# Reordering the opening of a fused attention and mixture-of-experts kernel: block-diagonal keys by one product, six staging rooms for the shared weights

## The reference, cut to what matters

```python
x = x + tanh(g_xattn[0]) * xattn(layernorm(x), ctx, ctx, W_q, b_q, W_k, b_k, W_v, b_v, W_o, b_o)
x = x + tanh(g_ffn[0]) * ffn(layernorm(x), ln_g, ln_b, Wr, W1, W3, W2, W1s, W3s, W2s)

# xattn
scores = einsum('bhsd,bhtd->bhst', qh, kh) / sqrt(16)
attn = einsum('bhst,bhtd->bhsd', softmax(scores), vh)      # then W_o and b_o
# ffn
h = layernorm(x, ln_g, ln_b)
gates, idx = top 2 of softmax(h @ Wr)                       # routed part, capacity 732 slots per expert
shared = silu(h @ W1s) * (h @ W3s) @ W2s
out = routed + shared
```

## Time and profile before

| | |
|---|---|
| time, median of 3 runs | 896.01 us (895.62 to 900.38) |
| profiled execution, its own time | 895.07 us |
| its span from first to last instruction | 893.3 us |
| PE busy | 832.9 us, 93% |
| DVE busy | 587.8 us, 66% |
| ACT busy | 387.7 us, 43% |
| POOL busy | 329.8 us, 37% |
| mean granted TensorE clock | 0.982 of full |

### The profile page before, as it was taken

How to read it: one execution, slowest core, us unless ns; L and a number is a source line. 1 busy time by engine, 2 the same in 40 slices (tenths; PEclk the granted TensorE clock), 3 DMA queues, 4 the chain that set the end, 5 groups by cost and what they waited for, 6 DMA issues and landing times.

```text
span 893.3 us, 14663 instructions
## 1 busy us (share of the span) xinstructions
PE 832.9 (93%) x5262; PEld 725.7 (81%) x5262; DVE 587.8 (66%) x1284; ACT 387.7 (43%) x717; POOL 329.8 (37%) x251
## 2 busy tenths in 40 slices
PE   8788999999989999999998999999999999999990
PEld 7464876858857778588587899999999999999990
DVE  4576769777588686795777577565666757565340
ACT  4336345363353442633525245453544445353330
POOL 4841203232032230230225812818466481814333
PEclk9899999999999999999899999999999999999995
DMA  6641310422204114131032422434444333431111
GB/s 222 163 111 34 94 37 25 119 48 62 71 25 117 18 37 112 36 78 31 24 118 72 139 83 62 94 106 88 83 111 91 99 61 87 100 65 20 18 19 19
DMA packets 93985, 66.94 MB, mean 75 GB/s; under 512 B 55110, under 2 KB 80892, under 8 KB 93928
## 3 DMA queue, kind: packets, MB, share of 16 engines
q1 hardware_dynamic: 40312, 55.40, 21.9%
q0 software_dynamic: 53088, 10.30, 8.4%
q10 hardware_dynamic: 528, 0.52, 0.2%
HBM read 37.38 MB, written 14.27 MB: 58 GB/s over the span
## 4 chain that ended last, share of the span: by engine, by line
PE 70%; DVE 12%; issue 6%; ACT 3%; POOL 2%; DVEq 0%; POOLq 0%; ACTq 0%
PE bank L1574 19%; PE bank L1575 18%; PE bank L1576 18%; PE bank L1802 2%; DVE row_max L1260 2%; PE bank L1803 2%; PE bank L1804 2%; PE bank L1664 2%; PE bank L1692 2%; DVE hidden L1343 1%; ACT float_data L1080 1%; DVE hidden L1278 1%; PE bank L1698 1%; PE bank L1844 1%; PE bank L1767 1%
## 5 line engine op out<-in xcount | busy, mean ns | idle before, releaser
L1574 PE MATMUL bank<-split_operands 128*128 128x366 f32 (+4 forms) x1148 | 382.0, 333 | 9.3 <-DVE float_data L1296 4.4
L1575 PE MATMUL bank<-split_operands 128*128 128x366 f32 (+4 forms) x1148 | 376.3, 328 | 0.0
L1576 PE MATMUL bank<-split_operands 128*128 128x366 f32 (+4 forms) x1148 | 376.1, 328 | 0.0
L1574 PEld LDWEIGHTS bank<-split_operands 128*128 128x128 f32 (+1 forms) x1148 | 214.5, 187 | 29.4 <-issue 8.2
L1576 PEld LDWEIGHTS bank<-split_operands 128*128 128x128 f32 (+1 forms) x1148 | 214.1, 186 | 12.1
L1575 PEld LDWEIGHTS bank<-split_operands 128*128 128x128 f32 (+1 forms) x1148 | 214.5, 187 | 9.5
L998 POOL DMA_INDIRECT out<-float_data,scatter_now x42 | 125.4, 2987 | 179.6 <-DVE float_data L1537 97.6
L1557 DVE TENSOR_TENSOR hidden<-bank,float_data 128x366 f32<-128x366 f32 x112 | 60.5, 540 | 114.1 <-PE bank L1576 114.1
L1179 ACT ACTIVATE float_data<-bank 128x366 f32<-128x366 f32 x112 | 53.5, 478 | 113.7 <-PE bank L1576 113.7
L1176 ACT CAST split_operands<-hidden 128x366 fp32r<-128x366 f32 x112 | 55.7, 497 | 68.3 <-DVE hidden L1557 68.3
L973 POOL DMA_INDIRECT float_data<-z_scratch,gather_now x42 | 72.2, 1720 | 14.8 <-issue 14.2
(11 more groups left out here) (157 smaller groups left out, 1066.8 us busy)
## 6 DMA issues: line engine op xcount, KB each, us to landing
float_data<-in_L_ffn_W SPq DMA_DIRECT2D x21, 1024.0 KB, 8.3
split_operands<-split_operands SPq DMA_DIRECT2D x96, 128.0 KB, 2.3
float_data<-in_x SPq DMA_DIRECT2D x8, 512.0 KB, 4.6
z_scratch<-float_data SPq DMA_DIRECT2D x8, 512.0 KB, 3.2
out<-float_data SPq DMA_DIRECT2D x7, 512.0 KB, 2.9
split_operands<-split_operands SPq DMA_DIRECT2D x8, 192.0 KB, 3.8
float_data<-in_L_ffn_W1s SPq DMA_DIRECT2D x2, 512.0 KB, 9.5
float_data<-in_L_ffn_W3s SPq DMA_DIRECT2D x2, 512.0 KB, 7.8
```

What stands on the lines that cost most here:

```text
L1574: pe.matmul(o, lhs[0], rhs[0], start=first, stop=False)
L1575: pe.matmul(o, lhs[0], rhs[1], start=False, stop=False)
L1576: return pe.matmul(o, lhs[1], rhs[0], start=False, stop=last)
```

## The change

In words, all in the opening:

- The eight DMAs of `first_keys` that fill `kbd`, and POOL's clearing of `kbd`, go. In their place POOL builds a 128 x 8 mask `own_head` with three small instructions (1 where the row belongs to the head), and DVE writes all of `kbd` by one product of the keys with the mask (`spread_keys`, 1232 columns), after `transpose_x` of block 0.
- Each of the six halves has a room of its own: `prob[2]`, `prob[3]`, `gf` and three in the float area. Halves 3 to 5 are issued without waits (`more_shared`), right behind the key stores and ahead of the `kst` reads.
- ACT rounds all twelve shared pieces in one run before the maxima are done. Two runs of pieces, of four and of two, leave their places between the exponentials and behind `attention_hi`. POOL takes the first six remainders ahead of `residual`, the other six behind the second block's statistics and values, and then `residual` of block 0. `residual` of block 1 and `route_const` move behind `attention_lo`.
- `stats_x` of block 1 comes ahead of `values_out`.
- `project_values` moves from between the maxima 2 and 3 to behind them. Maxima 0 waits for the hi part of the queries (`qh_ready`) and the product, no longer for the lo part; the banks of even and odd tiles are exchanged.
- New waits: the exponentials 2 and 3, the first DVE step of `scores` and `project_out` each wait for the POOL remainders that still read their room.

```diff
@@ def first_period(do, b):
     do("bias_keys")
+    do("more_shared")
     do("transpose_x", b)
+    do("spread_keys")
...
-    do("residual", b)
     do("stack", b)
-    do("shared_weights")
+    do("shared_hi", 0, 6)
+    do("shared_lo", 0, 6)
     for t in range(TT):
         do("maxima", b, t)
         if t == 1:
             do("keep_busy", 6, 4, "xl_ready", KD)
-        if t == 2:
-            do("project_values")
+    do("project_values")
...
-    do("more_shared")
+    do("stats_x", n)
     do("values_out")
-    norm(do, n)
+    do("shared_lo", 6, NPIECE)
+    do("scale_x", n)
+    do("residual", b)
     do("first_scores", b)
     do("transpose_x", n)
-    do("route_const")
     do("scores", b, 0)
-    do("shared_hi", 3, 5)
-    do("shared_lo", 6, 10)
...
     do("project", b)
-    do("shared_hi", 5, 6)
-    do("shared_lo", 10, NPIECE)
+    do("residual", n)
+    do("route_const")
     do("project_out", b)
@@ build
-    sh_stage = [af(kb, WCOLS // 2) for kb in (32, 40, 28, 32, 40, 44)]
+    sh_stage = [v.rearrange("p a n -> p (a n)") for v in (prob[2], prob[3], gf)] + \
+        [af(kb, WCOLS // 2) for kb in (32, 40, 28)]
+    own_head = sb("rows_of_head", [P, 8])
@@ sync, first_keys
-            sp.wait_ge(sig["zeros_ready"], 1)
-            sp.wait_ge(sig["k_hi"], KD)
-            for j in range(8):
-                sp.dma_start(kbd[16 * j:16 * j + 16, :, j, :].bitcast(F32), k_s[16 * j:16 * j + 16, 0, :, 0:SK].bitcast(F32))\
-                  .then_inc(sig["kbd_loaded"], 16)
             sp.wait_ge(sig["k_lo"], KD)
@@ vector
+        def spread_keys():
+
+            dve.wait_ge(sig["heads_ready"], 1)
+            dve.wait_ge(sig["k_hi"], KD)
+            dve.tensor_tensor(kbd, k_s[:, 0, :, 0:SK].bitcast(F32).unsqueeze(2).broadcast_to([P, KD, 8, SK]),
+                              own_head[:, :].unsqueeze(1).unsqueeze(3).broadcast_to([P, KD, 8, SK]), ALU.mult)\
+               .then_inc(sig["kbd_spread"], 1)
@@ tensor, maxima of block 0
-                    pe.wait_ge(sig["ql_ready"], KD)
-                    pe.wait_ge(sig["kbd_loaded"], 128)
+                    pe.wait_ge(sig["qh_ready"], KD)
+                    pe.wait_ge(sig["kbd_spread"], 1)
```

More of the change, by code:

```diff
@@ L464, in max_banks @@
     if b.at(0):
-        return (0, 1, 2) if t % 2 else (3, 4, 5)
+        return (3, 4, 5) if t % 2 else (0, 1, 2)
     if b.at(1):
@@ L651, in build @@
     stage_loaded = [sig["stage_loaded0"], sig["stage_loaded1"]]
-    shared_loaded = [sig[f"shared_loaded{j}"] for j in range(3)]
+    shared_loaded = [sig[f"shared_loaded{j}"] for j in range(6)]
     x_loaded = [sig["x_loaded0"], sig["x_loaded1"]]
@@ L704, in _, with load_shared @@
         sp.dma_start(xb[1], x_rows[1]).then_inc(x_loaded[1], 16)
-        def load_shared(h):
-            if h >= 3:
-                sp.wait_ge(sig["wsplit_lo"], NSTEP0 + 2 * (h - 2))
-            if h == 5:
-                sp.wait_ge(sig["xT_ready"], 2 * KD)
-            m, part = h // 2, h % 2
-            kk = wsv[m].shape[1] // 2
-            sp.dma_start(sh_stage[h].rearrange("p (k f) -> p k f", k=kk), wsv[m][:, part * kk:(part + 1) * kk])\
-              .then_inc(shared_loaded[h % 3], 16)
-        for h in range(3):
-            load_shared(h)
-        def first_keys():
-            sp.wait_ge(sig["zeros_ready"], 1)
-            sp.wait_ge(sig["k_hi"], KD)
-            for j in range(8):
-                sp.dma_start(kbd[16 * j:16 * j + 16, :, j, :].bitcast(F32), k_s[16 * j:16 * j + 16, 0, :, 0:SK].bitcast(F32))\
-                  .then_inc(sig["kbd_loaded"], 16)
+        def load_shared(first, last):
+            for h in range(first, last):
+                m, part = h // 2, h % 2
+                kk = wsv[m].shape[1] // 2
+                sp.dma_start(sh_stage[h].rearrange("p (k f) -> p k f", k=kk), wsv[m][:, part * kk:(part + 1) * kk])\
+                  .then_inc(shared_loaded[h], 16)
+        load_shared(0, 3)
+        def first_keys():
             sp.wait_ge(sig["k_lo"], KD)
@@ L731, in more_shared @@
         def more_shared():
-            for h in range(3, 6):
-                load_shared(h)
+            load_shared(3, 6)
         def load_keys(b):
@@ L744, in load_keys @@
                           .then_inc(sig["kbd_loaded"], 16)
+                if b.at(0):
+                    sp.wait_ge(sig["zeros_ready"], 1)
                 sp.wait_ge(sig["k_stored"], 32)
@@ L833, in _ @@
                            pattern=[[-1, P]], channel_multiplier=1).then_inc(sig["ident_ready"], 1)
-        do(pool.memset(kbd.bitcast(F32), 0.0))
+        do(pool.memset(own_head[:, :], 1.0))
+        do(pool.affine_select(out=own_head[:, :], in_=own_head[:, :], compare_op=ALU.is_ge, fill=0.0, base=0,
+                              pattern=[[-DH, 8]], channel_multiplier=1))
+        pool.affine_select(out=own_head[:, :], in_=own_head[:, :], compare_op=ALU.is_ge, fill=0.0, base=DH - 1,
+                           pattern=[[DH, 8]], channel_multiplier=-1).then_inc(sig["heads_ready"], 1)
         kneg = kst[96:112].rearrange("p a b t -> p (a b) t")
@@ L980, in first_gather @@
             gather(Turn(0, 1))
-        token_blocks(pool, {"stats_x": stats_x, "residual": residual, "weights": weights, "shared_weights": shared_weights,
+        token_blocks(pool, {"stats_x": stats_x, "residual": residual, "weights": weights,
                             "shared_lo": split_shared, "values_out": first_values, "scores": attention_lo, "stack": stationary_values, "norm2": norm2,
@@ L1037, in split_shared @@
         def split_shared(h):
-            act.wait_ge(shared_loaded[h % 3], 16 * (h // 3 + 1))
+            act.wait_ge(shared_loaded[h], 16)
             for j in range(2):
@@ L1043, in split_shared, with shared_hi @@
                    .then_inc(sig["wsplit_hi"], 1)
-        def shared_weights():
+        def shared_hi(first, last):
             act.activation(tgx[:, :], gx, ACT.Tanh).then_inc(sig["tanh_done"], 1)
             act.activation(tgf[:, :], gy, ACT.Tanh).then_inc(sig["tanh_done"], 1)
-            for h in range(3):
-                split_shared(h)
-        def shared_hi(first, last):
             for h in range(first, last):
@@ L1075, in exps @@
                 act.wait_ge(sig["wsplit_lo"], NSTEP0)
+            if b.at(0) and (p == 2 or p == 3):
+                act.wait_ge(sig["wsplit_lo"], NSTEP0 + 2 * (p - 1))
             act.wait_ge(sig["scores_ready"], b.n * NPAIR + p + 1)
@@ L1270, in scores @@
             dve.wait_ge(sig["z_stored"], b.n * 16)
+            if b.at(0):
+                dve.wait_ge(sig["wsplit_lo"], NSTEP0 + 6)
             if b.at(1):
@@ L1637, in maxima @@
                     pe.wait_ge(sig["k_lo"], KD)
+                    pe.wait_ge(sig["qh_ready"], KD)
+                    pe.wait_ge(sig["kbd_spread"], 1)
+                elif t == 1:
                     pe.wait_ge(sig["ql_ready"], KD)
-                    pe.wait_ge(sig["kbd_loaded"], 128)
-                elif t >= 2:
+                else:
                     pe.wait_ge(sig["m_done"], t - 1)
```

17 lines of the change are left out of this document (6 added, 11 removed).

## The result

| | before | after |
|---|---|---|
| median | 899.79 us (893.31 to 903.35, 22 runs) | 905.6 us (899.07 to 909.65, 22 runs) |
| ratio to before | | 1.0063, 95% interval 1.0039 to 1.0086 |
| profiled execution, its own time | 895.07 us, span 893.3 | 906.02 us, span 904.3 |
| mean granted clock in it | 0.982 | 0.970 |

The account below looks back on a forecast made before the run. The prediction took the opening's first scores on PE to be bound by SP's issue list, not by the maxima. It summed -2.4 us there and 0 for all else, from a median of 896.0 to 893.6 us, range 890.7 to 896.6.

Parts of the forecast that it names:

- T: Start of the first scores on PE, bound by SP's issue list: from 34.99 to 32.6 us, 2.4 earlier.
- Rival 2: New weight loads move in among the key stores, landing at 20.0 to 21.7: gain 0.9 to loss 0.8 us; chance 0.12.
- rival 1: Key stores land undisturbed at 17.1: gain 3.8 us, or 5.1 if the code load falls away too; chance 0.28.
- Rival 4: PE's slow clock lasts through the twelve query matmuls after the first scores: +2.9 us, 896.5; chance 0.03.
- cover: Rounded maxima ready at about 27.5, 1.5 us earlier and 2.7 before SP wants them: worth nothing.
- The product for `kbd`: On DVE after 14.6: 2.0 to 5.7 us, taken as 3, ending ahead of the hi queries; nothing reaches T.
- The casts: Four weight pieces, 2.18 us, leave ACT's place between the exponentials: worth 0.
- the step on POOL: Six remainders, block 1's normalisation at 30.4 instead of 35.4, six more until 36.8, residual until 39.6: slack, worth 0.
- + 0 (all else): Everything in the change besides the earlier first scores, summed as 0 us.
- My rival for the other side: The slower case: new loads delay the key stores, slower from a landing after 20.93, loss up to 0.8 us; chance 0.12.

Follow-up runs that it names:

- e4: Kernel before with only the block-diagonal keys changed (mask, one DVE product, eight copies gone), weight loads and pieces as before: 899.4 us, ratio to before 1.0028.
- e9: Kernel of e1 with only the first of six weight halves issued ahead of the key stores, the other five behind: 900.36 us, ratio to before 1.0000.
- e5: Kernel of e1 with 22 instead of 8 identity products on PE ahead of the first scores: 898.37 us, ratio to before 0.9992.
- e6: Kernel before with 27 instead of 8 identity products in PE's gap ahead of the first scores: 898.77 us, ratio to before 1.0019.
- e1: Changed kernel with POOL waiting for DVE's normalisation of block 1 before the second six weight remainders: 894.18 us, ratio to before 0.9975.
- e3: Changed kernel with POOL waiting for its own instruction behind each of the second six weight remainders: 899.56 us, ratio to before 1.0009.
- e8: Changed kernel with POOL's train cut after two of its ten instructions, waiting there for DVE's normalisation: 899.9 us in one run.
- e7: Changed kernel with PE's idle time ahead of the first scores and of block 1's transposes filled with identity products: 904.58 us, ratio to before 1.0058.
- e2: Changed kernel with block 1's normalisation as scalar_tensor_tensor with two tensor inputs, same order: 906.54 us, ratio to before 1.0074.
- e10: Kernel of e9 with 13 instead of 8 identity products ahead of the first scores: 898.37 us, ratio to before 0.9992.

## Why the prediction was wrong

**Right: what bounds T, and its size.** The reads were to start at 18.5 (17.8 to 19.5), it was 19.11; from there to T 14.06, it was 14.27, with one long issue in it as before (1.66 us at 21.39, again among the `kst` reads and not, as I had it, among the queries); T 32.6, it was 33.38. Rival 2 (new loads delay the stores) has e4 against it, rival 1 (undisturbed stores) e4 and e9. Rival 4 didn't come: the slow clock ended at about 43.6, and block 1's query products from 47.20 on ran at 1.00. The Trainium skill's rule on the order in which a DMA engine takes its descriptors ("DMA: Bandwidth & Descriptors", section "Queues, rings and completion order"), cited in the prediction, isn't contradicted: with loads issued behind them the stores took 5.8 to 6.8 us to the first read, without them 5.97.

**Right: cover and zeros.** The maxima were rounded at 28.07 (27.5), 2.9 us ahead of their copy. The product for `kbd` took 2.43 us (3, within 2.0 to 5.7) and held nobody. The casts are worth nothing (e5 against e6). And with POOL held back, in e1, the rest of the sum came out: first scores 2.1 us earlier than before, `project` 2.4, the time 0.25% less, 2.2 us against the 2.4 forecast, in an interval that just reaches no change.

**Wrong: the step on POOL.** It says that the statistics put first give "the normalised block at 30.4, not 35.4. Its transposes run behind the first scores, so this is slack too. Then six more until 36.8 and the residual". Start and end of POOL's train were right to about 0.5 us (29.93 to 37.31, then to 40.03); the start of the normalisation to 0.65 (29.65). What failed is its duration: I kept 1.38 us from a trace in which POOL was idle at that moment, and laid it beside ten POOL instructions. Two paragraphs above, for the `kbd` product, I had read from the earlier trace rows that a DVE instruction of 0.42 us takes 1.18 with POOL beside it. I used it there as a factor by columns, for the instruction that was new, and not for the instruction that was moved. The runs show it isn't a factor here: the normalisation, which works from SBUF to SBUF, waits for the end of what POOL runs, one instruction if POOL pauses behind it (e3), the whole train if it doesn't (e8, after). So this wait was 0 in the sum, part of its "+ 0 (all else)", and should have been: train end 40.03, less the 35.3 at which PE was free for the transposes, 4.7; measured 5.03.

The sum then: T 1.6 earlier; transposes 3.55 later than before, not 1.6 earlier, since they hang on POOL's train and no longer on T; `project` 4.1 later (58.30 against 54.22). The rest up to the measured 5.8 us I put down to the clock, which is argued and not shown: the fall in `project` costs 2.3 us where it comes, so 4.1 to 6.4 with it, but it comes with the old order too (e6), and how often in either kernel isn't known. The 10 us at 0.50 around the wait cost little (e7). In the two profiled executions the falls make the difference look like 11 us.

**The chances.** "Slower by more than 0.5%" had 0.02, and no rival of mine named a mechanism on POOL. My rival for the other side lay in the part that I had studied most. The order rows in front of the prediction show what it takes to see it: POOL's residual, which waited for the normalisation, had left its place between the statistics and the remainders, and with it went a wait that had kept the two engines apart by accident.

The Trainium skill states such a rule on the page "SBUF — State Buffer", section "SBUF: two separate sides": DVE and GpSimd share a pair of ports by an exclusive lock, which whichever starts first keeps for its whole instruction while the other stands still; DVE needs it in a two-port mode, and with two SBUF inputs when the GpSimd instruction reads SBUF. The trace agrees on who is held: L1236 and e2's form are, the reductions from PSUM are not. It doesn't give how long: with the pair kept for one instruction and then free, the first of the four would have waited 1.3 us, as in e3, and it waited 10.1.

**Left open.** Why DVE got in at a seam of POOL's train in some places (L1261 at 20.80 waited 0.63 us and then ran, with the train going on to 26.66; the 1.18 us of the earlier trace rows at 42.43 is such a place too, beside a train from 42.05 to 47.46) and at none of nine seams between 31.2 and 40.0. So the wait for the whole train is what this instruction met, and not a rule. Nor do the runs show what makes the clock fall in `project` or in the second period. PE stood idle for 2.28 us ahead of `project` in both profiles, and for 1.07 and 0.9 us ahead of the 17 us stretch and of its like before (at 82.30 and 84.69 after, 75.91 and 78.30 before), and the clock fell in one and not in the other.

## What to carry to other kernels

When a change moves work onto an engine that shares a path to memory with another, list what the other runs at that time and look up its duration beside such work, not alone; a wait that is removed may have been what kept them apart. If a train of POOL instructions has to run beside DVE work on the critical path, let it wait for that work, or give it a gap behind each instruction: one wait of 1.2 us was worth 6 to 8 here. A wait that is already met makes no gap. And behind a bound that is removed look for the next one on the same resource: the key stores gained 1.4 us in e9, and the way from the reads to the first scores lost 2.8 (13.45 to 16.27).

## What was not expected of the hardware

- Ten POOL `tensor_tensor` without a gap kept one DVE instruction of 0.40 us waiting for 10.1 us, two for 2.5; with a wait for its own end behind each, the two engines took turns, 1.26 and 0.1 us.
- The TensorE clock fell to 0.50 at `project` in nine of twelve profiles and for 17 us in the second period in six; both falls came with the old order (e6) and with the new. Identity products removed the fall ahead of the first scores in e5, e6 and e7, not in e10, and reliably no other.
- A DMA of 64 KB took 2.3 us from issue to landing in e1, with the engines at a share of 0.86 from 30 to 32 us, 4.3 in e9 (0.97) and 5.3 in e10 (1.06).
